# Grouped mixture of experts: indirect transfers with a bound on the row number, so that the rows of empty slots are skipped

## The chip, the cores and the metric

The kernel runs on 1 core of one Trainium2 chip. The metric is the device time of one execution in microseconds (us). It is a whole stack of four attention and feed-forward layers in one program; the change touches one of its stages.

## What is computed

The stage is the feed-forward part of the third layer (L2_ffn). With 1024 tokens of 256 values (x, normalized), 64 experts of width 176, of which each token uses 6, and a shared expert:

```
router_logits = x @ gate_w.T
probs = softmax(router_logits)
topk_w, topk_idx = top_k(probs, 6);  topk_w = topk_w / sum(topk_w)
combine = sum(one_hot(topk_idx, 64) * topk_w, axis=1)
h = silu(einsum('th,eih->tei', x, experts_w1))      # 64 experts, width 176
y = einsum('tei,ehi->teh', h, experts_w2)
routed_out = einsum('teh,te->th', y, combine)
g, u = split(x @ shared_gate_up.T)
shared_out = silu(g) * u @ shared_down.T
return routed_out + shared_out
```

All is float32. Only the 6 chosen experts of a token have a weight other than zero, so 1024 x 6 = 6144 pairs of a token and an expert need computing.

## The kernel before

`grouped_mixture` (L1957) sorts the pairs by expert into slots. Each expert's pairs start at a new block of 128 slots, and there are always 48 + 63 = 111 blocks (`BLOCKS`, L1912), since a program can't know how many each expert gets. The 111 x 128 = 14,208 slots hold the 6144 pairs; the rest are empty, at the end of each expert's last block and in whole blocks at the end.

**Before the loop.** The normalized tokens x_n are written to the DRAM tensor x_rows (L2061). Router, ranks within experts and one-hot matrices lead to one matmul group into place_bank (L2184), which holds for each slot 1 + 8 t + k, with the token t and the pair's place k, and 0 where the slot is empty. DVE makes of it `target`, the row of y_rows to which the slot's result goes (8 t + k, L2385), and `table`, the row of x_rows that the slot reads (target shifted right by 3, L2386, and cut to at most 1023, L2387). An empty slot gets a target of its own from `spare`, 8192 + 128 b + p (L2384), a row behind the 8192 that count, and by the cut it reads row 1023.

**The loop over 111 blocks b.** Five queues run side by side and meet at semaphores:

- SP loads the block's weights from DRAM into one of 6 slots: w (L2069, 304 KB) and w_rest (L2072, 48 KB). The expert's number is read from owner_row. It waits until the down matmuls of block b - 6 are done.
- POOL gathers the block's 128 token rows, `gather(b)` (L2284), into one of 6 slots of x_rows_of, once PE has turned the block b - 6; and it scatters the results, `scatter(b)` (L2289), once ACT has kept y. It issues gather(b) and then scatter(b - 9), in this order. A DMA_INDIRECT takes one row number per partition, from a column of `table` or `target`, and moves one row of 256 values (1 KB) for each.
- PE does turn(b + 2), the two transposes of the gathered rows (L2139), up(b + 1), the matmuls by the first weights (L2151), and down(b), those by the second (L2159, L2160), in this order. At six blocks it also does a unit of the shared expert (`late_in`, L2120), at four others `late_out` (L2131).
- DVE copies the turned rows from PSUM to x_t (L2409), and does small work of the weighting and the shared expert between.
- ACT applies Silu to the up result (h, L2240 and L2241) and then copies the y of the block before from PSUM (L2247). Before it overwrites a slot of y it waits for the scatter six blocks earlier.

**After the loop.** SP waits for all scatters and loads the 6 results of each token into y_of (8 loads, L2078, 768 KB each). PE and DVE weigh and add them to x.

On POOL's queue the stage begins with four iotas, a memset of w_rest (L2260) and one of a half of h (L2261), and then the norm's power (L191), from which DVE computes x_n (L180).

Of the kernel before, what the change touches and what calls it, by code (L numbers as in the profile page):

```python
# [14 lines left out]
F32 = mybir.dt.float32  # L15
# [4 lines left out]
P = 128  # L20
BATCH = 4
TOKENS = 1024
TT = TOKENS // P
D = 256
# [13 lines left out]
def wait_for(engine, semaphore, count):  # L38

    if not isinstance(count, int) or count > 0:  # L40
        engine.wait_ge(semaphore, count)
# [1915 lines left out]
def grouped_mixture(nc, m, dram, name):  # L1957
    of = Grouped
    experts, chosen, blocks, rest_of = of.EXPERTS, of.CHOSEN, of.BLOCKS, of.REST
    x_rows = nc.dram_tensor(name + "_x_rows", (TOKENS, D), F32, kind="Internal").ap()  # L1960
    y_rows = nc.dram_tensor(name + "_y_rows", (TOKENS * of.SPREAD + blocks * P, D), F32, kind="Internal").ap()
    w2_rows = dram["w"].rearrange("t p n -> (t p) n").rearrange("(e k) n -> e k n", k=of.WIDTH)
    pairs = TOKENS // (2 * P)
    shared_units = pairs * of.SHARED
    I32 = mybir.dt.int32

    with Stage(nc, m, name) as st:
# [35 lines left out]
        of_block = hots[:, TT * chosen * P:TT * chosen * (P + blocks)].rearrange("p (n b) -> p n b", b=blocks)  # L2003
        empty = st.sbuf("empty", [P, blocks])
        target = st.sbuf("target", [P, blocks], I32)
        source_i = st.sbuf("source_i", [P, blocks], I32)
        table = st.sbuf("table", [P, blocks], I32)
        equal = st.sbuf("equal", [P, 2, TT, experts])
        weight = st.sbuf("weight", [P, TT, 8])
# [8 lines left out]
        x_rows_of = st.sbuf("x_rows_of", [P, of.X_SLOTS, D])  # L2018
# [20 lines left out]
        gathered = [st.sem(f"gathered{n}") for n in range(of.X_SLOTS)]  # L2039
        y_stored = [st.sem(f"y_stored{n}") for n in range(of.Y_SLOTS)]  # L2040
        part_done, padded = st.sems("part_done", "padded")
# [11 lines left out]
        with st.block() as block:  # L2053

            @block.sync
            def _(sp):
                sp.dma_start(gate_w[:], dram["gate_w"].rearrange("(c p) n -> p c n", p=P)).then_inc(loaded, 16)
                sp.dma_start(before_raw[:], dram["before"]).then_inc(loaded, 16)
                sp.dma_start(shared_w[:], dram["shared_w"].rearrange("u p n -> p u n")).then_inc(shared_loaded, 16)
                sp.wait_ge(norm.xn_done, TT)  # L2060
                sp.dma_start(x_rows.rearrange("(t p) d -> p t d", p=P), m.x_n[:]).then_inc(x_stored, 16)  # L2061
                sp.wait_ge(m.repacked, m.repack_count)
                sp.wait_ge(owner_kept, 1)

                for b in range(blocks):
                    slot = b % of.W_SLOTS
                    e = sp.value_load(owner_row[0:1, b:b + 1], min_val=0, max_val=experts - 1)
                    wait_for(sp, y_ready, b - of.W_SLOTS + 1)
                    sp.dma_start(w[:, slot, :], m.w_rows[bass.ds(e, 1)].rearrange("e p n -> p (e n)")).then_inc(w_loaded[slot], 16)  # L2069
                    if b == 0:  # L2070
                        sp.wait_ge(padded, 2)
                    sp.dma_start(w_rest[0:rest_of, slot, :], w2_rows[bass.ds(e, 1)].rearrange("e k n -> k (e n)")[P:of.WIDTH, D:2 * D]  # L2072
                                 ).then_inc(w_loaded[slot], 16)
                for n in range(of.Y_SLOTS):
                    sp.wait_ge(y_stored[n], 16 * len(range(n, blocks, of.Y_SLOTS)))
                returns = y_rows[0:TOKENS * of.SPREAD, :].rearrange("(t p k) d -> t p k d", p=P, k=of.SPREAD)
                for t in range(TT):
                    sp.dma_start(y_of[:, t, :, :], returns[t, :, 0:chosen, :]).then_inc(returned[t], 16)  # L2078
# [174 lines left out]
            @block.gpsimd  # L2253
            def _(pool):
                pool.iota(row_i[:], pattern=[[1, P]], base=0, channel_multiplier=0).then_inc(counters_set, 1)
                pool.iota(column_i[:, 0:1], pattern=[[0, 1]], base=0, channel_multiplier=1).then_inc(counters_set, 1)
                pool.iota(spare_i[:], pattern=[[P, blocks]], base=TOKENS * of.SPREAD + 1, channel_multiplier=1).then_inc(counters_set, 1)
                pool.iota(column_i[:, 1:1 + TT * chosen].rearrange("p (t k) -> p t k", t=TT), pattern=[[P * of.SPREAD, TT], [1, chosen]],
                          base=1, channel_multiplier=of.SPREAD).then_inc(counters_set, 1)
                pool.memset(w_rest[:], 0.0).then_inc(padded, 1)  # L2260
                pool.memset(h[:, :, 1, :], 0.0).then_inc(padded, 1)  # L2261
                norm.gpsimd(pool)

                def shared_multiply(pair):
                    for u in range(of.SHARED):
                        n = pair * of.SHARED + u
                        pool.wait_ge(pair_kept, n + 1)
                        wait_for(pool, shared_y_ready, 2 * (pair - 1) if u == 0 else 0)
                        pool.tensor_tensor(shared_h[:, pair % 2, u, :], shared_gate[:, n % 2, :], shared_up[:, n % 2, :],
                                           ALU.mult).then_inc(shared_h_done, 1)  # L2270

                shared_multiply(0)
                shared_multiply(1)
                pool.wait_ge(part_done, 1)
                for t in range(TT):
                    for k in range(of.POOL_HOTS):
                        pool.tensor_scalar(in_block[:, t * chosen + k, :], row[:], part[:, 0, t * 8 + k:t * 8 + k + 1], None,
                                           ALU.is_equal).then_inc(pool_hots, 1)
                pool.wait_ge(x_stored, 16)
                pool.wait_ge(table_kept, 1)  # L2280

                def gather(b):
                    wait_for(pool, x_turned, b - of.X_SLOTS + 1)
                    pool.indirect_dma_start(x_rows_of[:, b % of.X_SLOTS, :], None, x_rows,  # L2284
                                            bass.IndirectOffsetOnAxis(table[:, b:b + 1], 0)).then_inc(gathered[b % of.X_SLOTS], 16)

                def scatter(b):
                    pool.wait_ge(y_kept, b + 1)
                    pool.indirect_dma_start(y_rows, bass.IndirectOffsetOnAxis(target[:, b:b + 1], 0), y[:, b % of.Y_SLOTS, :],  # L2289
                                            None).then_inc(y_stored[b % of.Y_SLOTS], 16)  # L2290

                for b in range(blocks + of.Y_LAG):
                    if b < blocks:
                        gather(b)
                    if b >= of.Y_LAG:
                        scatter(b - of.Y_LAG)

            @block.vector
            def _(dve):
# [3 lines left out]
                def link(instruction):  # L2303

                    nonlocal links
                    links += 1
                    instruction.then_inc(own, 1)
                    dve.wait_ge(own, links)
# [74 lines left out]
                dve.wait_ge(table_ready, 1)  # L2383
                link(dve.scalar_tensor_tensor(empty[:], place_bank[:, 0:blocks], 0.0, spare[:], ALU.is_equal, ALU.mult))  # L2384
                link(dve.scalar_tensor_tensor(target[:], place_bank[:, 0:blocks], -1.0, empty[:], ALU.add, ALU.add))  # L2385
                link(dve.tensor_scalar(source_i[:], target[:], 3, None, ALU.arith_shift_right))  # L2386
                dve.tensor_scalar(table[:], source_i[:], float(TOKENS - 1), None, ALU.min).then_inc(table_kept, 1)  # L2387

                steps = 0

# [498 lines left out]
```

## Time and profile before

| | us |
|---|---|
| Median of 3 runs | 2422.72 |
| Lowest and highest run | 2420.63, 2422.86 |
| Span of the profiled execution | 2416.4 |
| PE busy in it | 2108.2 (87%) |
| POOL busy in it | 774.1 (32%) |
| L2284 DMA_INDIRECT (gather), 111 | 108.2 busy |
| L2289 DMA_INDIRECT (scatter), 111 | 109.7 busy |

The profiled execution is known by its span, from the first to the last instruction. A run's time has some us around the span: the median of the runs is 6.3 us above it. Engines are PE (TensorE matmul), PEld (its weight load), DVE (VectorE), ACT (ScalarE), POOL (GpSimd) and SP (SyncE). Busy time of POOL for a DMA_INDIRECT is that of the instruction on POOL, not of the transfer, which the 16 DMA engines do afterwards. Waits name the engine whose semaphore released the waiting one, or "remote" where the trace names no instruction, or "issue" where nothing in the trace was waited for.

### The profile page before, as it was taken

Reading aid. Unit: us, or ns where it says so; the run is one execution under the profiler, and the core shown is the slowest. Engines: PE = TensorE matmul, PEld = TensorE weight load, DVE = VectorE, ACT = ScalarE, POOL = GpSimd, SP = SyncE. Lnnn points to the kernel's source line nnn. Section 1 sums busy time; section 2 is a strip of 40 time slices with the busy share of each in tenths; the row PEclk is TensorE's granted clock in tenths of the full one; section 3 lists DMA queues with packets and bytes.
Section 4 is the critical chain, followed back from the end, with each engine's and each line's share of the span. In section 5 each row is a group of like instructions: output and inputs, shape, how many; then the busy total and the mean of one; then the engine's idle time right before and its main releaser. Section 6 shows DMA issues by size and latency. Waiting matters only on the chain. (4 is left out here: it accounts for less than half of the span.)

```text
span 2416.4 us, 43095 instructions
## 1 busy us (share of the span) xinstructions
PE 2108.2 (87%) x12471; PEld 1754.7 (73%) x12471; DVE 1579.8 (65%) x4466; ACT 1217.6 (50%) x3021; POOL 774.1 (32%) x1120
## 2 busy tenths in 40 slices
PE   5799978598999997499999968888778999996999
PEld 3555556476899995279899867777656999995887
DVE  6677848784777786577778863111137887885655
ACT  4788842274666664166666512222215666662333
POOL 4433312210333331223323156666632323311221
PEclk9777789799999998699999988998898999997999
DMA  1156020101222111000000026676761000003431
GB/s 62 43 112 188 0 88 1 65 1 44 73 72 70 50 65 56 17 22 20 13 20 20 1 81 190 200 206 191 204 226 36 16 20 20 20 1 109 118 111 50
DMA packets 135857, 175.05 MB, mean 72 GB/s; under 512 B 44780, under 2 KB 102100, under 8 KB 133048
## 3 DMA queue, kind: packets, MB, share of 16 engines
q1 hardware_dynamic: 124664, 141.33, 20.2%
q0 software_dynamic: 10656, 29.11, 3.9%
q10 hardware_dynamic: 416, 3.15, 0.3%
q8 instruction: 58, 0.95, 0.2%
q14 instruction: 63, 0.52, 0.1%
HBM read 156.62 MB, written 36.83 MB: 80 GB/s over the span
## 5 line engine op out<-in xcount | busy, mean ns | idle before, releaser
L2409 DVE COPY l2f_x_t<-bank 128x256 f32<-128x256 f32 x111 | 46.3, 423 | 272.4 <-PE bank L2139 127.3
L637 ACT ACTIVATE l1a_prob<-l1a_masked,l1a_shift,l1a_q_scale 128x512 f32<-128x512 f32 x128 | 104.4, 816 | 79.5 <-DVE l1a_shift L691 78.5
L2151 PE MATMUL bank<-l2f_x_t,l2f_w 128*128 128x128 f32 x888 | 129.4, 293 | 11.7 <-issue 11.7
L2284 POOL DMA_INDIRECT l2f_x_rows_of<-l2f_x_rows,l2f_table x111 | 108.2, 975 | 91.6 <-remote 31.6
L2240 ACT ACTIVATE l2f_h<-bank 128x128 f32<-128x128 f32 x111 | 30.8, 277 | 203.7 <-PE bank L2151 100.4
L637 ACT ACTIVATE l2a_prob<-l2a_masked,l2a_shift 128x512 f32<-128x512 f32 x128 | 92.7, 724 | 80.6 <-DVE l2a_shift L695 77.8
L637 ACT ACTIVATE l3a_prob<-l3a_masked,l3a_shift 128x512 f32<-128x512 f32 x128 | 92.7, 724 | 79.6 <-DVE l3a_shift L695 77.0
L2151 PEld LDWEIGHTS bank<-l2f_x_t,l2f_w 128*128 128x128 f32 x888 | 118.5, 207 | 16.6 <-issue 16.3
L1176 ACT ACTIVATE l0a_prob<-bank,l0a_shift 128x496 f32<-128x496 f32 (+1 forms) x256 | 122.7, 553 | 2.4 <-DVE l0a_shift L1200 2.3
L2289 POOL DMA_INDIRECT l2f_y_rows<-l2f_y,l2f_target x111 | 109.7, 988 | 37.7 <-issue 33.1
L2159 PE MATMUL bank<-l2f_w,l2f_h 128*128 128x256 f32 x222 | 76.6, 430 | 48.9 <-ACT l2f_h L2241 37.6
L1195 DVE TENSOR_REDUCE l0a_top<-bank 128x1 f32<-128x496 f32 (+1 forms) x256 | 90.1, 410 | 36.1 <-PE bank L1134 35.9
L685 DVE CUSTOM_DVE_ANT_0 l3a_masked<-bank,l3a_side 128x512 f32<-128x512 f32 x128 | 88.4, 691 | 16.4 <-issue 16.2
L685 DVE CUSTOM_DVE_ANT_0 l2a_masked<-bank,l2a_side 128x512 f32<-128x512 f32 x128 | 88.4, 691 | 16.0 <-issue 15.9
L685 DVE CUSTOM_DVE_ANT_0 l1a_masked<-bank,l1a_side 128x512 f32<-128x512 f32 x128 | 88.4, 691 | 14.9 <-issue 14.9
L2491 POOL TENSOR_TENSOR l3f_low<-l3f_raw,l3f_high 128x768 fp32r<-128x768 f32 x24 | 44.3, 1847 | 160.0 <-ACT l3f_high L2486 160.0
L1154 PEld LDWEIGHTS bank<-ident,l0a_prob 128*128 128x128 f32 x512 | 68.6, 167 | 30.2 <-issue 18.3
L1154 PE MATMUL bank<-ident,l0a_prob 128*128 128x128 f32 x512 | 87.7, 325 | 1.1 <-DVE l0a_prob L1209 0.3
L754 POOL TENSOR_TENSOR l2a_pool_woken<-ones 128x1 f32<-128x1 f32 x60 | 11.6, 193 | 229.1 <-ACT l2a_q_t L621 122.3
L754 POOL TENSOR_TENSOR l3a_pool_woken<-ones 128x1 f32<-128x1 f32 x60 | 11.6, 193 | 227.9 <-ACT l3a_q_t L621 121.4
L1134 PE MATMUL bank<-l0a_k_t,l0a_q_t 64*128 64x512 f32 x128 | 65.2, 567 | 21.2 <-ACT l0a_prob L1176 16.0
L2710 DVE TENSOR_TENSOR l3f_upped<-l3f_gate,bank 128x512 f32<-128x512 f32 x48 | 33.0, 687 | 77.4 <-PE bank L2611 77.4
(591 smaller groups left out, 7549.0 us busy)
## 6 DMA issues: line engine op xcount, KB each, us to landing
l2f_w<-w_rows SPq DMA_DIRECT2D x111, 304.0 KB
l1a_side<-rms SPq DMA_DIRECT2D x16, 1024.0 KB, 4.8
w_rows<-in_l2f_w SPq DMA_DIRECT2D x4, 2048.0 KB
l2f_hots<-l2f_y_rows SPq DMA_DIRECT2D x8, 768.0 KB, 10.0
l3f_raw<-in_l3f_w SPq DMA_DIRECT2D x24, 256.0 KB, 3.9
l3f_mix<-shares SPq DMA_DIRECT2D x16, 384.0 KB, 3.8
l2f_w_rest<-in_l2f_w SPq DMA_DIRECT2D x111, 48.0 KB
w_rows<-in_l2f_w SPq DMA_DIRECT2D x8, 512.0 KB
```

The source lines that it names most:

```text
L637: act.activation(prob[:, unit, :], masked[:, unit, :], ACT.Exp, bias=shift[:, unit:unit + 1], scale=q_scale[:, slot, t:t + 1] if qk_norm e ...
L685: dve.tensor_tensor_reduce(masked[:, unit, :], score_bank[q][:], side[:, slot if qk_norm else 0, b * KEYS:(b + 1) * KEYS], 1.0, LOWEST, AL ...
L1134: pe.matmul(score_bank[k % 2 * 2 + q][:], q_t[rows, slot, q * P:(q + 1) * P], k_t[rows, slot, :], start=True, stop=True).then_inc(scores_r ...
L1154: last = pe.transpose(turn_bank[q][:, n * P:(n + 1) * P], prob[:, (k - 3) % 4, q, n * P:(n + 1) * P], m.ident[:])
L1176: last = act.activation(prob[:, at, q, first:end], score_bank[at % 2 * 2 + q][:, first:end], ACT.Exp, bias=shift[:, at, q, part:part + 1], ...
L1195: last = dve.tensor_reduce(top[:, at, q, part:part + 1], score_bank[k % 2 * 2 + q][:, first:end], AX_X, ALU.max)
L2151: last = pe.matmul(pair_bank[b % 2][:, n * P:(n + 1) * P], w[:, slot, first:first + P], x_t[:, b % 2, c * P:(c + 1) * P], start=(c == 0), ...
L2159: pe.matmul(y_bank[b % 2][:, 0:D], h[:, b % 2, 0, :], w[:, slot, DC * of.WIDTH:of.ROW], start=True, stop=False)
L2284: pool.indirect_dma_start(x_rows_of[:, b % of.X_SLOTS, :], None, x_rows, bass.IndirectOffsetOnAxis(table[:, b:b + 1], 0)).then_inc(gathere ...
L2289: pool.indirect_dma_start(y_rows, bass.IndirectOffsetOnAxis(target[:, b:b + 1], 0), y[:, b % of.Y_SLOTS, :], None).then_inc(y_stored[b % o ...
L2409: dve.tensor_copy(x_t[:, b % 2, :], turn_bank[b % 2][:, 0:D]).then_inc(x_kept, 1)
L2491: pool.tensor_tensor(self.low[:, slot, at], self.raw[:, slot, at], self.high[:, slot, at].bitcast(F32), ALU.subtract).then_inc(self.low_do ...
```

## The change

Both indirect transfers get a bound on the row number, and rows above it are skipped without an error. The bound of the gather is 1023, of the scatter 8191. The cut of `table` to 1023 is dropped, so that an empty slot's row number (1024 and above, since its target is 8192 and above) lies over both bounds. A slot of x_rows_of whose row is skipped keeps what was there, so x_rows_of is set to zero once at the start. y_rows loses its spare rows.

```diff
-    y_rows = nc.dram_tensor(name + "_y_rows", (TOKENS * of.SPREAD + blocks * P, D), F32, kind="Internal").ap()
+    y_rows = nc.dram_tensor(name + "_y_rows", (TOKENS * of.SPREAD, D), F32, kind="Internal").ap()
...
-        source_i = st.sbuf("source_i", [P, blocks], I32)
...
                 pool.memset(h[:, :, 1, :], 0.0).then_inc(padded, 1)
+                pool.memset(x_rows_of[:], 0.0).then_inc(padded, 1)
                 norm.gpsimd(pool)
...
                 pool.wait_ge(table_kept, 1)
+                pool.wait_ge(padded, 3)
...
                     pool.indirect_dma_start(x_rows_of[:, b % of.X_SLOTS, :], None, x_rows,
-                                            bass.IndirectOffsetOnAxis(table[:, b:b + 1], 0)).then_inc(gathered[b % of.X_SLOTS], 16)
+                                            bass.IndirectOffsetOnAxis(table[:, b:b + 1], 0), bounds_check=TOKENS - 1,
+                                            oob_is_err=False).then_inc(gathered[b % of.X_SLOTS], 16)
...
                     pool.indirect_dma_start(y_rows, bass.IndirectOffsetOnAxis(target[:, b:b + 1], 0), y[:, b % of.Y_SLOTS, :],
-                                            None).then_inc(y_stored[b % of.Y_SLOTS], 16)
+                                            None, bounds_check=TOKENS * of.SPREAD - 1, oob_is_err=False).then_inc(y_stored[b % of.Y_SLOTS], 16)
...
                 link(dve.scalar_tensor_tensor(target[:], place_bank[:, 0:blocks], -1.0, empty[:], ALU.add, ALU.add))
-                link(dve.tensor_scalar(source_i[:], target[:], 3, None, ALU.arith_shift_right))
-                dve.tensor_scalar(table[:], source_i[:], float(TOKENS - 1), None, ALU.min).then_inc(table_kept, 1)
+                dve.tensor_scalar(table[:], target[:], 3, None, ALU.arith_shift_right).then_inc(table_kept, 1)
```

## Rows read from the trace of the kernel before

**Rows 1.** The page's slices of the span: transfer engines busy, in tenths.

```profile
DMA  1156020101222111000000026676761000003431
```

**Rows 2.** Source lines L2284 and L2289: duration min/median/max, first and last start.

```profile
L2284 POOL DMA_INDIRECT l2f_x_rows_of<-l2f_x_rows,l2f_table x111: 942/970/1369, 1446.7 to 1772.6; - x111
...
L2289 POOL DMA_INDIRECT l2f_y_rows<-l2f_y,l2f_target x111: 969/988/1025, 1459.6 to 1789.2; - x111
```

**Rows 3.** Windows view, the loop: length, busy of each engine, clock, DMA share, GB/s.

```profile
1446.70:1790.20 343.50, 276.50 (x1626) 242.40 (x1626) 66.29 (x167) 84.94 (x339) 217.90 (x222) 0.90 0.67 196
```

**Rows 4.** Waits of POOL in the loop: us in total, times, longest us.

```profile
POOL l2f_x_rows_of L2284 <- remote: 31.6, 21, 2.2
POOL l2f_x_rows_of L2284 <- PE bank L2139: 31.2, 24, 2.9
```

**Rows 5.** Groups of PE in the loop: busy us, mean ns, idle before.

```profile
L2139 PE MATMUL bank<-ident,l2f_x_rows_of 128*128 128x128 f32 x222 | 46.3, 293 | 6.3 <-DMA l2f_x_rows_of<-l2f_x_rows,l2f_table 6.3
L2120 PE MATMUL bank<-l2g_x_t,l2f_shared_w 128*128 128x256 f32 x48 | 12.9, 417 | 0.0
```

**Rows 6.** Timelines of PE, ACT, POOL, 1699 to 1709 us: start, length, idle before.

```profile
1699.81 1.06 PE L2151 MATMUL bank<-l2f_x_t,l2f_w 128*128 128x128 f32 x8
...
1701.79 1.06 PE L2151 MATMUL bank<-l2f_x_t,l2f_w 128*128 128x128 f32 x8
...
1708.38 1.22 PE L2159 MATMUL bank<-l2f_w,l2f_h 128*128 128x256 f32 x2 [3.16 <-ACT l2f_h L2241]
...
1707.89 0.28 ACT L2240 ACTIVATE l2f_h<-bank 128x128 f32<-128x128 f32 x1 [4.69 <-remote]
...
1703.07 0.99 POOL L2289 DMA_INDIRECT l2f_y_rows<-l2f_y,l2f_target  x1 [0.30 <-issue]
```

**Rows 7.** The loop's end: a window, and ACT's timeline.

```profile
1780.00:1782.00 2.00, 2.00 (x16) 1.85 (x16) 0.45 (x2) 0.80 (x3) 1.57 (x2) 1.00 0.68 223
...
1782.68 0.28 ACT L2240 ACTIVATE l2f_h<-bank 128x128 f32<-128x128 f32 x1 [0.74 <-PE bank L2151]
...
1784.66 0.28 ACT L2240 ACTIVATE l2f_h<-bank 128x128 f32<-128x128 f32 x1 [0.33 <-PE bank L2151]
```

**Rows 8.** DMA queues in the loop: packets, MB, share of 16 engines.

```profile
q1 hardware_dynamic: 21840, 37.86, 39.4%
q0 software_dynamic: 10608, 28.98, 27.2%
```

**Rows 9.** Timelines of POOL and DVE at the stage's start.

```profile
1390.15 0.13 POOL L2256 IOTA l2f_column_i<- 128x1 int32 x1
...
1390.57 1.39 POOL L2260 MEMSET l2f_w_rest<- 128x1536 f32 x1
...
1392.18 2.15 POOL L191 TENSOR_TENSOR l2f_norm_rstd<-l2f_norm_spread,minus_half 128x4 f32<-128x4 f32 x2
...
1390.47 0.17 DVE L166 TENSOR_SCALAR l2f_norm_spread<-l2f_norm_moments 128x4 f32<-128x4 f32 x1
...
1393.23 2.67 DVE L180 TENSOR_SCALAR l2g_x_n<-x,l2f_norm_moments,l2f_norm_rstd 128x256 f32<-128x256 f32 x8 [0.67 <-POOL l2f_norm_rstd L191]
```

**Rows 10.** Timeline from the slots' table to the first turn.

```profile
1445.30 0.22 DVE L2386 TENSOR_SCALAR l2f_source_i<-l2f_target 128x111 int32<-128x111 int32 x1
...
1446.67 1.24 POOL L2284 DMA_INDIRECT l2f_x_rows_of<-l2f_x_rows,l2f_table  x1 [3.67 <-DVE l2f_table L2387]
...
1449.87 0.66 PE L2139 MATMUL bank<-ident,l2f_x_rows_of 128*128 128x128 f32 x2 [5.22 <-DMA l2f_x_rows_of<-l2f_x_rows,l2f_table]
```

**Rows 11.** ACT's copies of the first, the 77th and the last y.

```profile
1458.03 0.37 ACT L2247 COPY l2f_y<-bank 128x256 f32<-128x256 f32 x1 [1.96 <-remote]
...
1693.08 0.37 ACT L2247 COPY l2f_y<-bank 128x256 f32<-128x256 f32 x1 [1.03 <-PE bank L2160]
...
1788.15 0.37 ACT L2247 COPY l2f_y<-bank 128x256 f32<-128x256 f32 x1 [0.49 <-PE bank L2160]
```

**Rows 12.** POOL's compares of 128x128 ahead of the loop.

```profile
L2277 POOL TENSOR_SCALAR l2f_hots<-l2f_row,l2f_part 128x128 f32<-128x128 f32 x32 | 20.4, 656 | 2.8 <-DVE l2f_part L2371 2.8
```

## The prediction

> **What bounds the kernel now.** I began with the page's 40 slices of 60 us, to find the stage. Only slices 25 to 30, from about 1450 us on, have the transfer engines busy at 6 to 7 tenths [rows 1], and the 222 DMA_INDIRECT of lines L2284 and L2289 stand there [rows 2]. The windows view gives their stretch as one row: 343.5 us, PE busy 276.5, POOL 217.9, transfers 0.67 of 16 engines [rows 3]. The profiled span is 2416.4 us, the median of the runs 2422.72 us; I keep the 6.3 us between them as it is and sum against the span.
>
> Which wait ends last in the loop? POOL has 222 transfers to issue, one gather and one scatter for each of 111 blocks. Back to back that is 0.97 or 0.99 us of work and 0.30 of gap, 1.28 us [rows 2, 6]. So POOL alone needs 222 x 1.28 = 284 us. The loop takes 59 us more. The waits view of POOL says where: 31.6 us before gathers, put down to remote, and 31.2 us to PE's turn L2139 [rows 4]; a gather waits for nothing but that turn, so both are PE. PE alone would need less still: its block takes 1.98 us where it runs freely (L2151 at 1699.81 and again at 1701.79), so 111 x 1.98 = 220, and with the shared matmuls L2120 (12.9) 233 us [rows 5, 6]. Neither engine is full. The loop stops at irregular places for both.
>
> The timeline shows what such a stop is. The matmuls L2151 of one block are recorded from 1701.79 to 1702.85, and ACT needs nothing else for its L2240. It starts it at 1707.89; PE goes on with what it can, then stands for 3.16 us before its L2159 [rows 6]. Taken at their word, these records say that PE's completion reached ACT 5.0 us late. Data is not late: PE waited visibly for a gathered tile only 6.3 us in all [rows 5]. In the last blocks, after the last gather (1772.6) [rows 2], weights and scatters still move at 223 GB/s, but ACT's starts come 1.98 us apart and no such stop is left [rows 7]. So the stops go with indirect traffic, and with gathers above all; whether with their rows or with the issuing itself, this trace does not say. That is the main unknown.
>
> **How many rows go.** The loop has 111 x 128 = 14,208 slots and 1024 x 6 = 6144 pairs: 8064 slots, 57%, are empty. Counting the router's choices of the reference on its inputs and rounding each expert up to 128 gives 76 blocks with pairs (63% full) and 35 at the end that are wholly empty. A block moves 304 + 48 KB of weights and 128 + 128 KB by indirect transfers, 608 KB. After the change it is 352 + 0.63 x 256 = 514 KB in blocks 0 to 75, and 352 KB in the last 35. The software queue now takes 27.2 points of the engines' 67, beside the 39.4 of the hardware queue [rows 8]; 57% of that is 15 points.
>
> **What it changes, part by part.**
> The memset of x_rows_of is 128x1536, as w_rest's, which took 1.39 us. It stands on POOL ahead of the norm's power. POOL is already late there: DVE had the first spread at 1390.47 + 0.17, the power L191 began at 1392.18, and DVE's x_n waited for it until 1393.23 [rows 9]. Everything of the stage follows from x_n, so I count +1.3 us in full.
> On DVE one instruction of 0.22 us (0.26 with its link) goes between PE's table and the first gather, which nothing covers: -0.3 us [rows 10]. The added wait for padded stands on POOL where it has been met for 50 us: 0. Behind it are queued the gathers, which wait for the table anyway. Weight loads on SP, the scatters' order and all buffers are as before; stale rows in a slot cost PE the same as fresh ones. The eight loads of y_of after the last scatter read the same 6 MB: 0.
> The indirect transfers are the sum. Two prices aren't in the trace.
> (a) The stops. ACT copies the first y at 1458.03, the 77th at 1693.08 and the last at 1788.15 [rows 11], so a block takes 235.1/76 = 3.09 us in the first part and 95.1/34 = 2.80 in the last, against POOL's 2.56. The excess is 0.53 x 76 = 40 and 0.24 x 34 = 8 us; the other 11 are start and end. Least: nothing goes, if stops come from the issuing. Most: all 48 us go, and POOL's pace is next. In proportion to the rows, 37% of the 40 and all of the 8 go, 23 us. At the end of the loop 223 GB/s flow beside PE without a stop, so the stops look like something that sets in above a load and not in proportion to it; I take 35, the middle of 23 and 48. Once they go, POOL's own pace is late next.
> (b) The length of one DMA_INDIRECT. It may grow by a comparison of each index or shrink by what isn't written. The nearest rows for growth are POOL's own small operations, 0.13 us for 128x1 and 0.66 us for a compare of 128x128 [rows 9, 12]; for shrinking, at most 57% of 0.97, 0.55 us. I take 0, nearest to what the 222 show: 0.942, 0.970 and 1.369 us for the shortest, the median and the longest gather, 0.969 to 1.025 for scatters [rows 2], with one price for full blocks and for empty ones.
> Sum: +1.3 - 0.3 - 35 = -34, so 2422.7 - 34 = 2389 us.
>
> The Trainium skill, DMA: Bandwidth & Descriptors, Anatomy of one DMA — SWDGE (gpsimd) path, gives one such transfer about 2.0 us fixed plus its bytes at 436 GB/s. That makes 2.3 us for 128 KB and, as an estimate, 2.1 with 57% of it gone. The first gather here was used 3.2 us after its issue (1446.67 to 1449.87) [rows 10], more than the rule but of its kind. It speaks for rival 1.
> The skill's Perfetto Trace Analysis, DMA Instruction — SWDGE (GPSIMD), says that the recorded end is the writing of the last descriptor. By it the 0.97 us is generation, and fewer descriptors would shorten it; it speaks for rival 3, and no row here has a transfer with fewer.
>
> **The rivals.**
> 1. Nothing moves. The stops come from POOL's issuing, or the skipped rows still pass as packets. For it: data is never late in the loop, six slots of lead (over 10 us) cover the landing, and the transfer engines have a third of their time free. Against it: the stops are gone where the gathers are. Time: +1.0, 2424 us.
> 2. Slower: POOL becomes the bound by a longer issue. All 222 run on one engine, in order. It has 59 us of slack, so it decides from 59/222 = 0.27 us more for each. With 0.40 us, the middle of 0.13 and 0.66, the loop is 222 x 1.68 = 373 us plus some 3 at the start, +32: 2455 us. With 0.66 it is 222 x 1.94 = 431, +87: 2511 us. With 0.13 it is 313, and the gain is still 28. For it: comparing the row numbers with a bound, and leaving some out, is work that isn't done now. Against it: only that nothing here shows it.
> 3. Much faster: the issue gets shorter with the rows, stops vanish, and PE becomes the bound. At 233 to 250 us for the loop this is 94 to 110 less, 2314 to 2330 us; it needs an issue shorter by 0.15 us, 222 x 1.13 = 251. With half of that, 268 us, it is 2348.
>
> **How the numbers follow.** The forecast (2375 to 2401 us by its own range, the proportional 23 and the full 48) gets 0.36, and small gains from there down to 0.2% 0.07. Rival 3 gets 0.11, rival 1 0.16, rival 2 with all its prices that show 0.30. A difference of less than about 0.2%, 5 us, can't be told from none here. So faster 0.54, same 0.16, slower 0.30. The range for 8 in 10 reaches down to rival 3's half, 2348, and up over rival 2's middle to 2462; a longer issue than 0.43 us stays outside it.
>
> **What would show it.** Right: both DMA_INDIRECT groups stay at 0.97 to 0.99 us; bytes of the software queue fall from 29 MB to about 12.6 (43%); POOL's waits for PE's turns shrink from 63 to about 30 us, the loop from 343.5 to about 308; blocks from 76 on at 2.56 to 2.6 us each. Wrong at (a): waits of POOL and ACT as now. Wrong at (b): the mean of L2284 or L2289 away from 0.98 us, in full and empty blocks alike or in the empty ones alone, and idle time of POOL gone. If the power L191 does not begin 1.3 us later after the stage's start, the memset was mis-sized.

## The result and the profile after

The changed kernel took 2426.4 us (median of 10 runs, 2424.5 to 2432.0), the kernel before 2415.6 us (10 runs, 2406.0 to 2422.9). The ratio is 1.0047, interval [1.0035, 1.006]: 0.47% slower, 11 us, where 34 us less were forecast. The profiled execution of after has a span of 2428.3 us. Single executions of one kernel lie up to 17 us apart, so the loops of two traces compare roughly, and the medians decide.

The transfers carry what was forecast. The view of the transfer queues in the loop, kernel after (packets, MB, share of 16 engines), against [rows 8]:

```profile
q1 hardware_dynamic: 21840, 37.86, 37.3%
q0 software_dynamic: 10608, 12.66, 11.9%
```

The software queue moves 12.66 MB instead of 28.98, and its share falls from 27.2 to 11.9 points. The number of packets stays 10608: 3,980 of the whole kernel's packets now have 16 bytes where all had 4096 or 4 before, and each covers four skipped rows. By these sizes a skipped row passes as 4 bytes instead of 1024; it does not vanish.

The loop didn't get shorter. The windows view of it, kernel after (length; busy of PE, weight load, DVE, ACT, POOL; clock; DMA share; GB/s), against [rows 3]:

```profile
1450.56:1801.90 351.34, 277.48 (x1626) 241.84 (x1626) 66.29 (x167) 86.56 (x339) 228.40 (x222) 0.90 0.50 145
```

It is 351.3 us instead of 343.5, with 145 GB/s instead of 196, at the same granted clock of 0.90. POOL's busy time grew by 10.5 us. The source lines of the two transfers (duration min/median/max, ns; first and last start) say how, against [rows 2]:

```profile
L2285 POOL DMA_INDIRECT l2f_x_rows_of<-l2f_x_rows,l2f_table x111: 997/1029/1308, 1450.6 to 1782.5; - x111
...
L2291 POOL DMA_INDIRECT l2f_y_rows<-l2f_y,l2f_target x111: 980/1017/1339, 1464.1 to 1800.8; - x111
```

A gather is 0.06 us longer and a scatter 0.03, in blocks with pairs (1.040 and 1.023 us in the mean) as in the wholly empty ones (1.028 and 1.011). POOL's waits in the loop (us in total, times, longest), against the 62.8 us of [rows 4]:

```profile
POOL l2f_x_rows_of L2285 <- ACT l2f_y L2246: 29.3, 16, 2.0
...
POOL l2f_x_rows_of L2285 <- PE bank L2138: 20.6, 11, 3.1
POOL l2f_x_rows_of L2285 <- remote: 8.8, 5, 1.9
```

That is 58.7 us; half of 63 was forecast. The stops of [rows 6] are still there, in the wholly empty blocks too. The timeline of one, kernel after (start, length, idle before):

```profile
1739.09 1.06 PE L2150 MATMUL bank<-l2f_x_t,l2f_w 128*128 128x128 f32 x8
...
1745.04 0.28 ACT L2239 ACTIVATE l2f_h<-bank 128x128 f32<-128x128 f32 x1 [5.34 <-remote]
1745.15 0.42 DVE L2410 COPY l2f_x_t<-bank 128x256 f32<-128x256 f32 x1 [3.76 <-remote]
...
1745.53 0.70 PE L2158 MATMUL bank<-l2f_w,l2f_h 128*128 128x256 f32 x2 [3.11 <-ACT l2f_h L2240]
```

L2150 is recorded as over at 1740.15, and the ACT instruction that needs nothing else starts at 1745.04. Below, a *late start* is a block whose first activation on ACT starts over 1 us after the recorded end of its matmuls: 57 of the 111 blocks in the trace before (2.7 us late in the median, 8.5 at most), 58 in the trace after (3.2 and 6.5). 18 of them lie in the 35 empty blocks in either trace. The traces show these times; that PE was done when its record says so is taken from the records.

The stage's start, kernel after, against [rows 9]:

```profile
1394.85 1.37 POOL L2261 MEMSET l2f_x_rows_of<- 128x1536 f32 x1
...
1396.20 2.15 POOL L191 TENSOR_TENSOR l2f_norm_rstd<-l2f_norm_spread,minus_half 128x4 f32<-128x4 f32 x2
...
1450.56 1.30 POOL L2285 DMA_INDIRECT l2f_x_rows_of<-l2f_x_rows,l2f_table  x1 [3.48 <-issue]
```

The power starts 4.02 us later than before; 2.70 of that the stage brought along from earlier stages, 1.32 is the memset. The first gather starts 3.89 us later.

### The profile page after: what moved, and what is told of

Same layout as the page of the kernel before. It is cut to its first block and busy times, and to the rows that moved or that the text cites. A ratio compares the mean times of both kernels' runs of the same rounds, so it can differ in the third digit from the quotient of the medians.

```text
span 2428.3 us, 43317 instructions
## 1 busy us (share of the span) xinstructions
PE 2112.8 (87%) x12471; PEld 1757.2 (72%) x12471; DVE 1580.8 (65%) x4465; ACT 1220.1 (50%) x3021; POOL 787.9 (32%) x1121
## 3 DMA queue, kind: packets, MB, share of 16 engines
q0 software_dynamic: 10656, 12.66, 1.7%
## 5 line engine op out<-in xcount | busy, mean ns | idle before, releaser
L2285 POOL DMA_INDIRECT l2f_x_rows_of<-l2f_x_rows,l2f_table x111 | 115.3, 1039 | 87.0 <-ACT l2f_y L2246 29.3
L2150 PE MATMUL bank<-l2f_x_t,l2f_w 128*128 128x128 f32 x888 | 128.2, 291 | 17.3 <-issue 17.1
L2150 PEld LDWEIGHTS bank<-l2f_x_t,l2f_w 128*128 128x128 f32 x888 | 116.9, 205 | 22.3 <-issue 22.2
```

The costliest lines, as they stand in the source:

```text
L2150: last = pe.matmul(pair_bank[b % 2][:, n * P:(n + 1) * P], w[:, slot, first:first + P], x_t[:, b % 2, c * P:(c + 1) * P], start=(c == 0), ...
```

## The experiments

All ratios are to the kernel before, measured in the same set of runs as the experiment. There are five sets, and in them the kernel before took: 2417.6 us (the four experiments on the bound, chip number 5), 2422.7 and 2414.4 us (the experiments on the stops, both chip number 4), 2365.6 us (the three shorter pauses, chip number 14) and 2364.9 us (the last three runs, chip number 5 again). A loop runs from the first gather to the end of the last scatter.

**What in the change costs.** The changed kernel with the gathers alone bounded, the scatters as before:

```
 gather:  ..., IndirectOffsetOnAxis(table[:, b:b + 1], 0), bounds_check=TOKENS - 1, oob_is_err=False)
-scatter: ..., None, bounds_check=TOKENS * of.SPREAD - 1, oob_is_err=False)
+scatter: ..., None)     # y_rows with its spare rows again
```

> Only the gathers have the bound; the scatters write the spare rows of empty slots as before. Theory A (each bounded transfer costs POOL a little more, and POOL's issuing paces the loop): gathers 1.04 us in the mean instead of 0.975, scatters 0.988 as before; 111 x 0.064 = 7 us at most on POOL, of which some 5 show, with the memset's 1.3: +6 us, ratio 1.0025. Theory B (the cost sits in the transfers that are skipped on the way to DRAM, scatters): ratio 1.0005, only the memset shows. Theory C (the 8 us of the loop are scatter between runs and no cost of the bound): 1.0005 as well, but with the longer gather on record.

2426.5 against 2417.6 us, ratio 1.0042 [1.0028, 1.0055]. The scatters alone, from the changed kernel:

```
-gather: ..., bounds_check=TOKENS - 1, oob_is_err=False)     +gather: ...)
-table = target >> 3                                         +table = min(target >> 3, TOKENS - 1)
-pool.memset(x_rows_of[:], 0.0), pool.wait_ge(padded, 3)
```

> Only the scatters have the bound, gathers read row 1023 for empty slots as before, no memset, the DVE instruction is back. Theory A: scatters 1.02 us in the mean instead of 0.988, 111 x 0.031 = 3.4 us at most, ratio 1.001. Theory B: ratio 1.003 to 1.004. Theory C: 1.000.

2415.0 us, 0.9994 [0.998, 1.0008]. Both with a bound that no row passes:

```
-table = target >> 3                      +table = min(target >> 3, TOKENS - 1)
-scatter bounds_check=TOKENS * SPREAD - 1 +scatter bounds_check=TOKENS * SPREAD + blocks * P - 1
-memset of x_rows_of, wait for padded     # and y_rows with its spare rows again
```

> Both transfers have a bound, but the row numbers are those of before, so no row is ever over it and all 29 MB move. No memset. If the comparison is what makes the instruction longer: gathers 1.04, scatters 1.02 in the mean, as in the changed kernel, and ratio 1.003 to 1.004 (loop +8 us without the fewer bytes). If skipping rows makes it longer: 0.975 and 0.988 as before, ratio 1.000.

2429.8 us, 1.0053 [1.0038, 1.0068]. POOL's groups (count, busy us, mean ns, idle before) of the gathers-only kernel, then of the bound never met:

```profile
L2285 POOL DMA_INDIRECT l2f_x_rows_of<-l2f_x_rows,l2f_table x111 | 115.7, 1042 | 77.7 <-issue 30.1 <-PE bank L2138 24.4 <-remote 23.3
L2291 POOL DMA_INDIRECT l2f_y_rows<-l2f_y,l2f_target x111 | 114.1, 1028 | 39.1 <-issue 31.2 <-ACT l2f_y L2246 7.3 <-PE bank L2138 0.6
```

```profile
L2284 POOL DMA_INDIRECT l2f_x_rows_of<-l2f_x_rows,l2f_table x111 | 115.0, 1036 | 85.2 <-ACT l2f_y L2247 32.5 <-issue 26.6 <-PE bank L2139 17.9
L2290 POOL DMA_INDIRECT l2f_y_rows<-l2f_y,l2f_target x111 | 113.6, 1023 | 40.4 <-issue 35.9 <-ACT l2f_y L2247 4.5
```

With all 29 MB moving and nothing skipped the cost is all there. So it is the bound itself that costs, by its longer instruction, and the skipping brings nothing that these intervals (1.0053 [1.0038, 1.0068] beside 1.0047 [1.0035, 1.006]) can show. Theory B falls with the first two: it is the gather's bound. In the gathers-only kernel the scatter, which has no bound, is longer too (1028 ns instead of 988), so POOL is busy 11.9 us longer there. The scatters-only kernel gives POOL 4.4 us more (gathers 987 ns in the mean, scatters 1016), and 4.4 us would be a ratio of 1.0018, above its interval; why this smaller growth didn't show is open.

The memset behind the norm's power:

```
-pool.memset(x_rows_of[:], 0.0).then_inc(padded, 1)
 norm.gpsimd(pool)
+pool.memset(x_rows_of[:], 0.0).then_inc(padded, 1)
```

> The changed kernel with the memset of x_rows_of behind the norm's power on POOL instead of ahead of it. If the memset's 1.37 us stood on the path in full, this is 1.3 us faster than the changed kernel: ratio 1.0042 where that had 1.0047, power L191 3.9 us before the place it has now relative to the first gather's 52.9 us distance. If the delay is hidden further on: the same ratio as the changed kernel, and the distance from POOL's first iota to the first gather stays 57.9 us instead of falling to 56.6.

2427.3 us, 1.0035 [1.0021, 1.0049]. From the first iota (1392.14) to the first gather (1449.72) it is 57.58 us, against 57.91 in the changed kernel. That is 0.3 us and not 1.3, but one pair of traces can't tell: the kernel before itself has 56.72 us in one trace and 57.76 in another. Over all traces with gathers on POOL the four with the memset ahead of the power have 57.91 to 59.04, 58.3 in the mean, and the other fifteen 56.55 to 57.90, 57.2 in the mean. The difference, 1.1 us, agrees with the forecast's 1.3 less 0.3. The medians of the moved memset and of the changed kernel are 2.9 us apart in ratio, with intervals that overlap.

**What the stops need.** The kernel before, with each block's rows by one direct transfer on SP's queue; the choice of the rows is left out:

```
 ...  # SP, per block: waits for x_rows and for PE's turn of block b - 6
+sp.dma_start(x_rows_of[:, b % of.X_SLOTS, :], x_rows[b % TT * P:(b % TT + 1) * P, :])
-    if b < blocks: gather(b)        # on POOL
```

> From the kernel before. Each block's 128 KB come by one direct transfer of 128 consecutive rows of x_rows on the hardware queue of SP; the choice of rows is left out. POOL issues only the 111 scatters. Bytes and packets of PE's side are as before. Theory A (POOL's issuing of indirect transfers makes both the pace and the stops): POOL needs 111 x 1.29 = 143 us, its pace is gone, the stops become fewer than half (40 gaps of over 3.6 us between the copies of y before), the loop falls from 343.5 to 235 to 290 us, 55 to 105 us less in all, ratio 0.957 to 0.977. Theory D (the stops come from all the traffic, whoever issues it): stops as before, loop over 320 us.

2318.4 against 2422.7 us, 0.9556 [0.9534, 0.9578], no late start. Its mirror, the scatters direct on SP's queue, six blocks behind the loads; the choice of the rows that they go to is left out:

```
 ...  # SP, per block: waits for ACT's copy of y
+sp.dma_start(y_rows[b % 64 * P:(b % 64 + 1) * P, :], y[:, b % of.Y_SLOTS, :])
-    if b >= of.Y_LAG: scatter(b - of.Y_LAG)        # on POOL
```

> From the kernel before, the mirror of the direct gathers: the gathers stay indirect on POOL, each scatter is one direct store of 128 KB on SP's queue (to which rows is left out). POOL then issues one transfer per block, 1.27 us, less than PE's 1.98. Theory P (PE outruns POOL's 2.56 us a block, runs dry, falls to the half clock, and POOL waits for it in turn): nothing to run dry of, stops under 10 of 40, loop 235 to 250 us, -95 to -105 us, ratio 0.957 to 0.961. Theory G (gathers by themselves hold PE's completions up): stops as before, loop over 290 us, ratio over 0.98.

2338.3 against 2414.4 us, 0.9694 [0.9673, 0.9714], one late start. Windows over nearly all of the direct gathers' loop and of the direct scatters':

```profile
1450.00:1690.00 240.00, 232.12 (x1592) 211.41 (x1590) 66.49 (x163) 90.41 (x334) 112.20 (x111) 0.99 0.89 279
```

```profile
1450.00:1708.00 258.00, 242.89 (x1626) 219.34 (x1626) 67.14 (x167) 91.14 (x339) 102.56 (x109) 0.99 0.91 260
```

At 279 and 260 GB/s, with the transfer engines 0.89 and 0.91 busy instead of 0.67, there are no stops: load alone doesn't make them. From first to last copy of y it is 234 and 248 us, 330 before. (Of the direct gathers' 104 us some 9 come from the first y, at 1449.1 instead of 1458.0, as they need no table.) Neither gathers nor scatters by POOL make stops where the others go direct. POOL then issues one indirect transfer a block instead of two, so it can be the mixture or the number of them in a stretch of time; no run tells these apart. From the other side, the kernel before without the loads of all weights but the first six blocks'; the other blocks' weights are left out:

```
 e = sp.value_load(...)
+if b >= of.W_SLOTS: continue
-pe.wait_ge(w_loaded[slot], 32 * (b // of.W_SLOTS + 1))
+pe.wait_ge(w_loaded[slot], 32)
```

> From the kernel before. Only the first six blocks' weights are loaded, later blocks use them again: the weights of the other blocks are left out. Gathers and scatters are as before and are the only traffic. Theory A: stops stay as they are (38 to 40 over 3.6 us), the loop stays within 10 us of 343.5, ratio 0.996 to 1.000. Theory D (load of the transfer engines): 39.4 of their 67 points go, the stops with them, loop 300 us or less, ratio 0.98 or less.

2413.1 us, 0.9959 [0.994, 0.9977], 51 late starts. The loop's window:

```profile
1448.11:1783.63 335.52, 273.98 (x1626) 239.19 (x1626) 66.42 (x167) 86.51 (x339) 218.59 (x222) 0.91 0.30 87
```

87 GB/s, and the stops are all there. The changed kernel with no transfer of POOL issued for blocks 76 to 110, a number that holds for these inputs (the waits for `gathered` and `y_stored` end at it too):

```
-if b < blocks: gather(b)        +if b < 76: gather(b)
-if b >= of.Y_LAG: scatter(...)  +if of.Y_LAG <= b < 76 + of.Y_LAG: scatter(...)
```

> From the changed kernel, but the gathers and scatters of blocks 76 to 110, which are wholly empty with these inputs, are not issued at all; PE and ACT compute these blocks as before. Theory A: the last 35 blocks run at PE's own 2.0 us instead of 2.9, -30 us against the changed kernel, ratio to before 0.992. Theory D (the stops come from weights and PE, not from the indirect transfers): the last 35 blocks stay above 2.6 us each, ratio 1.000 to 1.004.

2378.6 us, 0.9816 [0.9788, 0.9843], 48 us less than the changed kernel. The window of its last blocks:

```profile
1695.00:1760.00 65.00, 65.00 (x462) 60.02 (x460) 18.41 (x57) 26.47 (x99) 0.52 (x1) 1.00 0.68 203
```

PE never stands still, the granted clock is 1.00, no start is late behind block 75, and the last 35 copies of y come in 67.9 us, 1.94 each (100.4 in the changed kernel). By the two traces another 12.9 us are saved behind the loop: the first load of `y_of` is issued at 1752.0, ahead of the last copy of y (1761.3), where it stood behind the last scatter before.

**Whether a signal, slots or POOL's pace decides.** In the kernel before, the gather waits for DVE's copy of the turned tile instead of for PE's turn:

```
-wait_for(pool, x_turned, b - of.X_SLOTS + 1)
+wait_for(pool, x_kept, b - of.X_SLOTS + 1)
```

> From the kernel before. A gather waits for DVE's copy of the turned tile (x_kept) instead of PE's own turn (x_turned), so that POOL waits for no signal of PE; the wait comes some 0.5 us later. Theory S (PE's signals to POOL are what is held up, and hold the others): stops go, loop 290 to 310 us, ratio 0.98 to 0.99. Theories P and G: a slot comes free 0.5 us later, ratio 1.000 to 1.008.

1.0061 [1.0042, 1.0079], 56 late starts: POOL's waiting for PE's signal isn't the cause. Eight slots of rows, with five of weights so that both fit:

```
-W_SLOTS, X_SLOTS, Y_SLOTS = 6, 6, 6; Y_LAG = X_SLOTS + 3
+W_SLOTS, X_SLOTS, Y_SLOTS = 5, 8, 6; Y_LAG = 9
```

> From the kernel before: eight slots of gathered rows instead of six, and five of weights instead of six, so that both fit. Theory P: with two more blocks of lead POOL works on while PE is slow; its waits for PE's turns (63 us) fall to under 35, loop 310 to 325 us, ratio 0.987 to 0.993. Theory G (held-up completions come with the gathers, however many slots): POOL still waits over 50 us for PE's turns, ratio 0.998 to 1.002.

1.0051 [1.0034, 1.0067], 56 late starts. POOL's waits for PE's turns went (2.4 us are left), but came back at the next place, as the scatter is nine blocks behind as before. The waits of POOL in its loop:

```profile
POOL l2f_y_rows L2289 <- ACT l2f_y L2247: 69.6, 41, 2.7
```

So it says that slots don't remove the late starts, and not what a longer lag would do. A memset of 128x1 behind each gather:

```
+pool.memset(dose[:, b:b + 1], 0.0)
```

> From the kernel before, with one memset of 128x1 on POOL behind each gather, 0.1 us or less with its gap. No transfer changes. Theory A (POOL's pace is what the bound lengthened): the time grows by about as much as POOL is given more, 111 x 0.1 = 11 us at most, some 6 to 9 us, ratio 1.003 to 1.004. Theory E (POOL's waits absorb so little a growth, and the bound costs by what it does to the transfers): ratio 1.000 to 1.001.

0.9992 [0.9974, 1.0011]. It tests nothing: its 0.12 us lay wholly in the 0.30 us gap between two transfers, and the pace stayed 2.57 us. A longer one does stand out:

```
+if b >= 3: pool.memset(hots[:, b % 2 * 640:b % 2 * 640 + 640], 0.0).then_inc(dosed, 1)
```

> From the kernel before, with a memset of 128x640 on POOL behind each gather, about 0.57 us, more than the gap of 0.30 takes in, so POOL's two transfers and their gaps need about 3.0 us a block instead of 2.56. Theory P: POOL's pace counts in full though it is idle for 59 us of the loop, +35 to +55 us, ratio 1.014 to 1.023. If instead the stops come from transfers that follow each other without a pause, they go and the loop is 111 x 3.0 and some 8: 341 us, ratio 0.998 to 1.002.

2424.4 against 2414.4 us, 1.0043 [1.0026, 1.0059]. POOL got 0.53 us a block, 59 us, and the time grew by 10. Theory P missed by far. The other had the loop (341 forecast, 342.4 measured) and the stops, and its ratio, 0.998 to 1.002, was just too low. Late starts fell to 5, of 1.7 us at most. Its loop's window, and PE's waits for the gathers in it:

```profile
1449.95:1792.36 342.41, 259.85 (x1626) 216.59 (x1626) 68.95 (x167) 86.75 (x339) 289.18 (x330) 0.97 0.66 196
```

```profile
PE bank L2141 <- DMA l2f_x_rows_of<-l2f_x_rows,l2f_table: 77.7, 71, 5.1
```

This loop is paced by POOL throughout, 3.09 us a block (gathers at 1499.61 and 1502.70): PE waits 71 times, plainly, for a gather. What POOL got more is about what the stops took before. Would a smaller pause remove the stops and cost less? The same line with 160 and with 320 for 640, and 320 behind the scatter:

> From the kernel before, with a memset of 128x160 behind each gather, some 0.25 us, 0.1 more than the gap takes in: POOL's own pace is 2.69 us a block (2.56 before, 2.65 in the changed kernel, 3.09 with the memset of 128x640, where hardly a completion of PE was late). Theory Q (late completions of PE come when POOL issues two indirect transfers in less than some 2.7 to 3 us, and cost more than the pace): still there or fewer; if they go, the loop is 111 x 2.69 and 8: 307 us, ratio 0.985. If the pace alone counts and the late completions stay: +3 to +14 us, ratio 1.001 to 1.006.

> The same with 128x320, some 0.38 us: POOL's own pace is 2.81 us a block. Theory Q: few late completions of PE are left (under 20 starts of L2240 over 1 us late, from 57), the loop is 111 x 2.81 and 8: 320 us, 20 us less than before, ratio 0.990 to 0.993. If late completions stay as they are and the pace adds: ratio 1.003 to 1.010.

> The same memset of 128x320, behind each scatter instead of each gather; same pace of 2.81 us. If it is the number of indirect transfers in a stretch of time that counts, as the one behind the gather; if a pause between a gather and the scatter behind it is what helps, this one does nothing for the late completions: ratio 1.003 to 1.010 where the other is below 1.

1.0065 [1.0051, 1.0079], 1.0112 [1.0097, 1.0127] and 1.0124 [1.0108, 1.0139], with 4, 6 and 2 late starts. But in this set the kernel before took 2365.6 us (9 runs, 2362.5 to 2367.4), not 2414 to 2423. So the three tell nothing of how stops go before it is known whether the kernel before has any at 2365 us. The kernel before, the changed one and the pause of 160, all unchanged, in one more set:

> The kernel before, unchanged, for a profile of its own on this chip. In the last call it took 2366 us, on the chips of the others 2414 to 2423. Theory Q2 (late completions of PE are a property of some chips, and POOL's pace of 2.56 us is the bound where they are absent): where it takes 2366 us, the loop is 111 x 2.56 and 8, 292 us, under 10 starts of ACT's L2240 are over 1 us late (57 in the first trace) and PE waits over 30 us for gathers (6.3). Where it takes 2415 us, all as in the first trace. Theory R (the whole chip is faster, or other stages are): a loop over 330 us at 2366.

> The changed kernel, unchanged, on this chip. Theory Q2, where before takes 2366 us: POOL's pace rises by 0.055 + 0.03 us a block, 111 x 0.085 = 9.4 us, with the memset's 1.3 less 0.3: +10 us, ratio 1.0045. Where it takes 2415: ratio 1.0047 as recorded. Were it the fewer bytes that bring something once the late completions are gone: ratio 1.000 or less.

> The memset of 128x160 behind each gather once more. Where before takes 2366 us: ratio 1.0065 as in the last call. Where it takes 2415: 0.985 if the pause does away with the late completions, 1.001 to 1.006 if it doesn't, and the count of starts of L2242 over 1 us late says which (4 in the last call's trace of this kernel, 57 in the first trace of before).

The kernel before again took 2364.9 us (17 runs), its copy 0.9997 [0.9986, 1.0008], the changed kernel 2374.4 us, 1.0041 [1.0026, 1.0057], the pause 1.0062 [1.0045, 1.0079]; late starts 0, 3 and 7. The loop's window and PE's waits, kernel before in this set:

```profile
1448.55:1734.02 285.47, 251.84 (x1626) 215.68 (x1626) 68.62 (x167) 88.65 (x339) 218.08 (x222) 0.97 0.82 235
```

```profile
PE bank L2139 <- DMA l2f_x_rows_of<-l2f_x_rows,l2f_table: 31.7, 45, 5.1
```

The same instructions, the same 29 MB at 235 GB/s instead of 196, no stop: 285.5 us, which is 111 x 2.57. POOL's pace is the bound here. The changed kernel's loop and POOL's groups in this set:

```profile
1448.82:1743.68 294.86, 250.22 (x1626) 213.89 (x1626) 67.62 (x167) 87.51 (x339) 227.30 (x222) 0.98 0.62 173
```

```profile
L2285 POOL DMA_INDIRECT l2f_x_rows_of<-l2f_x_rows,l2f_table x111 | 114.5, 1031 | 38.2 <-issue 30.9 <-PE bank L2138 5.2 <-ACT l2f_y L2246 2.1
L2291 POOL DMA_INDIRECT l2f_y_rows<-l2f_y,l2f_target x111 | 112.8, 1016 | 34.0 <-issue 25.7 <-PE bank L2138 5.5 <-ACT l2f_y L2246 2.8
```

The loop is 9.4 us longer. The instructions' busy time grew from 218.1 to 227.3 us, 9.2: the whole of it. The pauses count in full as well: their loops take 298.8, 314.1 and 314.9 us, 13, 29 and 29 more, and their medians are 14, 27 and 28 us above before. Of Theory Q2's numbers the loop's length was off, 285 instead of 292; the late starts (0, under 10 forecast) and PE's waits for gathers (31.7 us, over 30 forecast) came as it said. Its first half, that late completions are a property of some chips, is not shown. The record gives chip number 5 to this set and to the one on the bound, where the kernel before took 2417.6 us; if the number names one chip, that chip was seen with stops and without. What the runs show is that each of the sets is wholly of one kind.

The two kinds differ in one thing more. A transfer that lands adds to its semaphore, 16 times by the counts below, and the trace records these additions. The gathers in the transfer view, kernel before, in the first trace and in this set (the second ends with the median time to landing, which the view gives only if all additions were recorded):

```profile
l2f_x_rows_of<-l2f_x_rows,l2f_table POOLq DMA_INDIRECT x111
```

```profile
l2f_x_rows_of<-l2f_x_rows,l2f_table POOLq DMA_INDIRECT x111, 4.6
```

Counted between the first and the last copy of y, the first trace holds 1931 additions by transfers for 422 transfers, which make 6752, and 464 of the engines' own 724. In this set it is 6668 of 6720 and 718 of 726. The same goes for every kernel: 98% or more of the transfers' additions are recorded in the two sets of 2365 us, 26 to 64% in all other traces. Outside the loop both kinds record the same share (94 and 95%). The direct gathers (61%), the direct scatters (64%) and the long pause (45%) are among the latter. So their runs were of the kind with stops, and that they had hardly any is their own doing. Whether what loses the records also holds PE's signals up, or the recording itself does both, no run tells.

## Why the prediction was wrong

**Step (a), -35 us for the stops: failed, it was 0.** The bytes fell to 12.66 MB (12.6 forecast), and the stops stayed: 58 late starts where there were 57. "The stops look like something that sets in above a load" is what failed. With 87 GB/s they are there (51 late starts), with 279 they aren't (none). The end of the loop [rows 7] had two things at once, no gathers and half of POOL's issues; I read the first as rows that no longer flow. Where gathers and scatters are both issued by POOL at 2.57 us a block, stops come in some sets of runs; with one of the two, or at 3.09 us, hardly any came there. Rival 1 had it: the stops don't follow the rows, and the skipped rows still pass as packets. It got 0.16, and the case for it, that data was never late, stood in the text. That its 2424 us lies so near the measured 2426.4 is luck: it was counted as 1.0 above 2422.7, the median of three runs, and ten runs gave 2415.6, so 10.9 us were measured against its 1.0.

**Step (b), 0 us: mis-sized, and by its own rule wrongly excused.** It measured +0.06 us for a gather and +0.03 for a scatter. The bounds (-0.55 to 0.66) held it. But the text let POOL absorb up to 0.27 us each in its 59 us of slack. In the sets with stops the price counted in full or nearly so: 1.0053, 12 us, for the bound alone with 10.7 us more of POOL, and +7.7 us of loop for 10.5 us of POOL in the first two traces; only the 4.4 us of the scatters' bound did not show. The 59 us weren't slack. In the trace before, 160 of the 221 gaps between POOL's transfers are the bare 0.30 us and the waiting stands in the others; my reading is that POOL's pace is the bound between the stops. Where there are no stops no slack is left, and that is shown: 9.2 us of instruction make 9.4 us of loop. Rival 2 had the sign and the place, at 0.40 us over eight times too dear. (Its 2511 us for 0.66 leaves out some 2 us of the start that its 2455 counts; nothing rests on it.)

**The memset, +1.3, and the DVE instruction, -0.3:** L191 began 1.32 us later, as said. The first gather came 3.89 us later, of which 2.70 is the stage's start; 1.2 is left, where 1.0 was forecast, and the 1.1 over all traces agrees. The two terms aren't told apart at the first gather, which moves by about 1 us between traces of one kernel.

The time after follows from these: +7.7 (loop) and about 1 (start) are 9 of the 11 us between the medians. The two profiled spans are 11.9 us apart, with 2.7 of that from earlier stages.

**What stays open.** Why the other engines start so late after PE's recorded ends, what differs between the sets of runs, and from which pace on the late starts go where they occur: the pauses of 160 and 320 columns only ran where there were none. Measured there, at a pace between 2.57 and 3.09 us, a small pause might win; no run shows it. No general version beat the kernel before. Not issuing the empty blocks' transfers, with the number of filled blocks fixed at 76 for these inputs, takes 1.8% off in a set with stops (interval 1.6 to 2.1%), so a POOL that read the number of blocks at run time could be worth it; that version wasn't run, and neither was this one without stops.

## What to carry to other kernels

A bound that skips rows saved bytes here and no instruction, packet or gap, and it made the issuing instruction longer on every transfer, skipped rows or not. So it can pay only where the bytes are what is late, which they weren't here. Idle time on an engine is slack only if it is there in each turn: ask what the engine does between its waits, and if it runs back to back there, what is added to each instruction can count in full. Before a wait is put down to load, look for a stretch with more load and no wait. Where a stage has waits that no row explains, profile the unchanged kernel again in another set of runs, and look at what the two traces recorded.

## What the runs showed of the hardware

- The kernel before took 2414 to 2423 us in the median of some sets of runs and 2365 in others, 2% apart, and by the two traces all of it is in one loop: 343.5 against 285.5 us, late starts 57 against 0, granted clock 0.90 against 0.97. Chip number 5 stands with both kinds in the record.
- In the first kind, ACT starts 1.1 to 8.5 us (2.7 in the median) after PE's recorded end in 57 of the 111 blocks of the kernel before while POOL issues gathers and scatters in turn, and DVE and POOL start late beside it; transfers run on meanwhile (weights until 1706.9 in the stop of [rows 6], which is from 1702.9 to 1707.9). In the loops of this kind 26 to 64% of the transfers' additions to semaphores are in the traces, in those of the other kind 98% and more.
- With a bound on the row number a gather takes 1031 to 1042 ns in the mean instead of 975, a scatter 1016 to 1023 instead of 988, whether rows are skipped or not. A skipped row of 1024 bytes passes as 4.
- A scatter without a bound is 1028 ns in the mean behind bounded gathers, 988 and 991 in the two traces of the kernel before.
- A 128x1 memset of 0.12 us on POOL between two indirect transfers costs nothing that shows (0.9992 [0.9974, 1.0011]): it lies in their gap of 0.30.
